# Second cross-attention: the values become TensorE's stationary operand, in four column tiles, and one matmul a pair adds and turns the partial results

## The reference, cut to what matters

```python
q = _fq_sym((x @ Wq + bq) * scale, axis=-1)     # 64 rows, 16 heads of 16
k = _fq_sym(k, axis=-1)                         # 6272 keys
v = _fq_sym(v, axis=2)
attn = softmax(einsum('bhqd,bhkd->bhqk', q, k))
attn = _fq_unsigned(attn, axis=-1)              # rounded to 255 steps of the row's maximum
out = einsum('bhqk,bhkd->bhqd', attn, v)
return out @ Wp + bp
```

## Time and profile before

| | us |
|---|---|
| median of three runs | 1012.08 (1010.8 to 1012.2) |
| the profiled execution's own time | 1010.85 |
| its span | 1009.0 |
| TensorE busy | 967.4 |
| VectorE busy | 714.2 |
| the stage of the change, first scores to `attended` | 293.1 to 372.2 |

### The profile page before, as it was taken

How to read it: one execution, slowest core, us unless ns; L and a number is a source line. 1 busy time by engine, 2 the same in 40 slices (tenths; PEclk the granted TensorE clock), 3 DMA queues, 4 the chain that set the end, 5 groups by cost and what they waited for, 6 DMA issues and landing times.

```text
span 1009.0 us, 20653 instructions
## 1 busy us (share of the span) xinstructions
PE 967.4 (96%) x7809; PEld 653.3 (65%) x7809; DVE 714.2 (71%) x1919; ACT 360.3 (36%) x629; POOL 163.4 (16%) x146
## 2 busy tenths in 40 slices
PE   9999999999799988998999999999999999998998
PEld 5676776776444554366777777777777777744555
DVE  5768776777789945788786767767676789753354
ACT  2332333324428841443343333333333343311211
POOL 0000000000210010234332323223322323000000
PEclk9999999999999989999999999999999999998999
DMA  8200100102439996990100000000000000413440
GB/s 319 75 22 23 40 21 21 42 5 85 151 127 183 192 300 240 352 315 3 41 12 1 2 0 0 0 0 0 0 0 0 0 22 22 168 63 99 165 179 3
DMA packets 70904, 82.99 MB, mean 82 GB/s; under 512 B 49728, under 2 KB 58176, under 8 KB 67008
## 3 DMA queue, kind: packets, MB, share of 16 engines
q1 hardware_dynamic: 70560, 82.17, 26.5%
q10 hardware_dynamic: 288, 0.07, 0.0%
HBM read 67.79 MB, written 2.42 MB: 70 GB/s over the span
## 4 chain that ended last, share of the span: by engine, by line
PE 76%; DVE 9%; issue 6%; DMA 3%; POOL 3%; ACT 3%; SPq 0%; POOLq 0%; DVEq 0%; PEld 0%; PEldq 0%
PE ps L2538 17%; PE ps L2429 13%; PE ps L2528 8%; PE ps L1682 8%; PE ps L1672 4%; PE ps L1693 4%; PE ps L1716 2%; PE ps L1728 2%; PE ps L532 2%; POOL x_sum L3114 2%; PE ps L3201 1%; DMA wide<-S 1%; DMA ring<-weights 1%; ACT S L2301 1%; PE ps L2452 1%
## 5 line engine op out<-in xcount | busy, mean ns | idle before, releaser
L2538 PE MATMUL ps<-vals,S 128*128 128x257 f32 x784 | 186.4, 381 | 1.0 <-ACT S L3043 1.0
L3114 POOL TENSOR_TENSOR x_sum<-x_max,consts 128x4 f32<-128x4 f32 (+1 forms) x104 | 136.1, 1309 | 298.6 <-DVE x_max L2748 298.6
L2538 PEld LDWEIGHTS ps<-vals,S 128*128 128x128 f32 x784 | 141.7, 190 | 18.8 <-issue 1.5
L2429 PE MATMUL ps<-keysT,row_biases_sb 128*128 128x512 f32 (+1 forms) x348 | 153.7, 568 | 0.0
L2760 DVE SCALAR_TENSOR_TENSOR S<-ps,x_sum,keysT 128x128 f32<-128x128 f32 x392 | 110.8, 344 | 55.4 <-PE ps L2538 50.9
L3043 ACT ACTIVATE S<-S 128x512 f32<-128x512 f32 (+1 forms) x104 | 62.6, 605 | 197.1 <-DVE S L2801 196.6
L2528 PE MATMUL ps<-x_q,x_keys 128*128 128x128 f32 x784 | 112.9, 286 | 0.0
L2528 PEld LDWEIGHTS ps<-x_q,x_keys 128*128 128x128 f32 x784 | 95.4, 191 | 0.1
L2429 PEld LDWEIGHTS ps<-keysT,row_biases_sb 128*128 128x128 f32 x348 | 62.8, 189 | 46.6 <-issue 41.9
L1682 PE MATMUL ps<-ring,S 128*128 128x512 f32 x196 | 92.4, 593 | 0.2
L1809 ACT ACTIVATE S<-ps 128x2048 f32<-128x2048 f32 (+1 forms) x25 | 46.1, 1844 | 82.7 <-PE ps L1728 76.5
(11 more groups left out here) (494 smaller groups left out, 1404.4 us busy)
## 6 DMA issues: line engine op xcount, KB each, us to landing
ring<-weights SPq DMA_DIRECT2D x24, 1024.0 KB, 6.9
keysT<-ctxT SPq DMA_DIRECT2D x2, 3136.0 KB, 15.8
vals<-ctxN SPq DMA_DIRECT2D x1, 6272.0 KB, 26.5
S<-ctxT SPq DMA_DIRECT2D x11, 512.0 KB, 4.0
ring<-weights SPq DMA_DIRECT2D x5, 768.0 KB, 6.0
kept_keys<-S SPq DMA_DIRECT2D x9, 256.0 KB, 2.7
x_keys<-kept_keys SPq DMA_DIRECT2D x9, 256.0 KB, 2.6
keysT<-weights SPq DMA_DIRECT2D x1, 1792.0 KB, 8.7
```

Source lines behind the costliest of these rows:

```text
L2429: ins = pe.matmul(ps[:, x2_key_bank(g, c), 0:width(c)], weights_of(g)[:, k, :], ctxT[:, k, span(c)], start=k == 0, stop=k == KT - 1)
L2538: ins = pe.matmul(bank(6, D + 1), S[:, a:a + TILE], ctx_and_ones[:, SUB * c + s, :], start=c == 0 and s == 0, stop=c == NC - 1 and s == su ...
L3114: pool.tensor_tensor(x2_inv[:, c % 2, 0:n], x2_var[:, c % 2, 0:n], C("neg_half").broadcast_to([128, n]), ALU.pow)\
```

## The change

In `weigh`, the stationary operand is now the pair's 32 value columns of a key tile (128 keys x 32) and the moving one the turned probabilities (128 keys x 128 queries). Key tile s goes to column tile s mod 4 of TensorE, that is to PSUM partitions 32 (s mod 4) and up. So four partial sums of 32 value columns x 128 queries stand below one another. The number of matmuls is the same.

`finish(j)` copies all 128 x 128 of them to one of two buffers `x1_parts`. A new TensorE step `fold(j)` takes this copy as stationary operand and `x1_fold` (four 32 x 32 identities below one another, f32) as the moving one: it adds the four partial sums and turns the result to 128 queries x 32, in its own place of bank 6 or 7. `fold(j-2)` stands ahead of `scores(j+1, 2)`, `fold(6)` inside `turn_last(2)`, and `fold(7)` after the last `weigh`. GpSimd makes `x1_fold` with two additions at the start of the stage. The last products read PSUM, and are four instead of two.

```diff
+            def fold(j):
+                pe.wait_ge(sem("x1_tile_done"), j + 1)
+                return pe.matmul(ps[:, 6 + j % 2, x1_own(j)], x1_parts[j % 2], x1_fold, start=True, stop=True)
...
             def turn_last(e):
...
                     if b == 6:
-                        pe.wait_ge(sem("x1_tile_done"), PAIRS - 1)
+                        fold(PAIRS - 2)
...
                 for s in range(n):
-                    ins = pe.matmul(ps[:, 6 + j % 2, 0:128], probsT[:, s, :], vals_int[:, x1_tile(e, s), 128 * (j // 4):128 * (j // 4) + 128],
-                                    start=e == 0 and s == 0, stop=e == PROB_GROUPS - 1 and s == n - 1)
+                    c = 32 * (s % 4)
+                    ins = pe.matmul(ps[c:c + 32, 6 + j % 2, 0:128], vals_int[:, x1_tile(e, s), 32 * j:32 * j + 32], probsT[:, s, :],
+                                    start=e == 0 and s < 4, stop=e == PROB_GROUPS - 1 and s >= n - 4, skip_group_check=True)
...
             pe.wait_ge(sem("values_narrowed"), 9)
+            pe.wait_ge(sem("x1_ident"), since("x1_ident", 3))
             for j in range(PAIRS):
                 if j == PAIRS - 1:
                     pe.wait_ge(sem("x1_scores"), since("x1_scores", PARTS * PAIRS))
+                if j >= 2:
+                    fold(j - 2)
...
             for e in (2, 3):
                 weigh(PAIRS - 1, e)
+            fold(PAIRS - 1).then_inc(sem("x1_weighed"), 1)
...
             def finish(j):
                 dve.wait_ge(sem("x1_weighed"), since("x1_weighed", PROB_GROUPS * (j + 1)))
-                dve.tensor_scalar(x1_out[:, 32 * j:32 * j + 32], ps[:, 6 + j % 2, 32 * (j % 4):32 * (j % 4) + 32], 2.0 ** 24, None, ALU.mult).then_inc(sem("x1_tile_done"), 1)
+                dve.tensor_scalar(x1_parts[j % 2], ps[:, 6 + j % 2, 0:128], 2.0 ** 24, None, ALU.mult).then_inc(sem("x1_tile_done"), 1)
...
-            dve.wait_ge(sem("x1_tile_done"), PAIRS)
+            dve.wait_ge(sem("x1_weighed"), since("x1_weighed", PROB_GROUPS * PAIRS + 1))
...
             for e in range(2):
                 rows_, cols_ = slice(T * e, T * e + T), slice(HD * e, HD * e + HD)
-                ins = dve.tensor_tensor(out[:, :, cols_], by_tile[rows_, :, cols_], step[rows_, :, cols_], ALU.mult)
+                for p in range(2):
+                    ins = dve.tensor_tensor(out[:, :, p, cols_], by_pair[rows_, :, p, cols_], step[rows_, :, p, cols_], ALU.mult)
...
+            pool.tensor_tensor(x1_fold64, C("ident")[:, 0:64], C("ident")[:, 64:128], ALU.add).then_inc(sem("x1_ident"), 1)
+            pool.wait_ge(sem("x1_ident"), since("x1_ident", 2))
+            pool.tensor_tensor(x1_fold, x1_fold64[:, 0:32], x1_fold64[:, 32:64], ALU.add).then_inc(sem("x1_ident"), 1)
```

More of the change, by code:

```diff
@@ L391, in perceiver @@
             "probsT_psum": (("x1_last_psum", 3, 7), ("x3_probsT_psum", 9, X3_PAIRS + 1)),
-            "probsT_ready": (("x1_ident", 3, 1), ("x3_probsT", 9, X3_PAIRS + 1)),
-            "weighed": (("x1_weighed", 3, PAIRS * PROB_GROUPS), ("x2_weighed", 6, GROUPS * NC), ("x3_weighed", 9, X3_PAIRS + 1)),
+            "probsT_ready": (("x1_ident", 3, 3), ("x3_probsT", 9, X3_PAIRS + 1)),
+            "weighed": (("x1_weighed", 3, PAIRS * PROB_GROUPS + 1), ("x2_weighed", 6, GROUPS * NC), ("x3_weighed", 9, X3_PAIRS + 1)),
             "tile_ready": (("x1_tile_ready", 3, 2), ("x2_tile_ready", 6, 2 * GROUPS)),
@@ L2031, in perceiver @@
         x1_queries = x2_probsT[:, :, :].rearrange("p a n -> p (a n)")
-        x1_q, x1_out = sw_key_both[0:T, 0, :], sw_key_both[:, 1, :]
+        x1_q = sw_key_both[0:T, 0, :]
+        x1_parts = [sw_key_both[:, 1, 128 * i:128 * i + 128] for i in range(2)]
+        x1_fold64, x1_fold = sw_value_part[:, 128:192], sw_value_part[:, 192:224]
         x1_q_rows = scratch(0, 1024, T)
@@ L2051, in x1_last_bank, with x1_own @@
             return 6 + (j + 1) % 2
+        def x1_own(j):
+            return slice(128 + 32 * (j // 2), 160 + 32 * (j // 2))
         def x1_probs(j, e):
@@ L2182, in x1_tensor @@
                     elif j + 1 == PAIRS:
-                        if e == 0:
-                            pe.wait_ge(sem("x1_ident"), since("x1_ident", 1))
                         turn_last(2 + e)
@@ L2280, in x1_vector @@
             finish(PAIRS - 1)
-            dve.wait_ge(sem("x1_tile_done"), PAIRS)
-            out, step = cut(attended[:, :], PAIRS, 32), cut(value_step[:, :], PAIRS, 32)
-            by_tile = cut(x1_out, PAIRS, 32)
+            dve.wait_ge(sem("x1_weighed"), since("x1_weighed", PROB_GROUPS * PAIRS + 1))
+            out = attended[:, :].rearrange("t (j p d) -> t j p d", p=2, d=32)
+            step = value_step[:, :].rearrange("t (j p d) -> t j p d", p=2, d=32)
+            by_pair = ps[:, 6:8, 128:256].rearrange("t p (j d) -> t j p d", d=32)
             for e in range(2):
                 rows_, cols_ = slice(T * e, T * e + T), slice(HD * e, HD * e + HD)
-                ins = dve.tensor_tensor(out[:, :, cols_], by_tile[rows_, :, cols_], step[rows_, :, cols_], ALU.mult)
+                for p in range(2):
+                    ins = dve.tensor_tensor(out[:, :, p, cols_], by_pair[rows_, :, p, cols_], step[rows_, :, p, cols_], ALU.mult)
             ins.then_inc(sem("attended"), 1)
```

## The result

The median went from 1011.44 us (four executions of each kernel, 1010.45 to 1012.2) to 1021.0 (1020.38 to 1022.49): 0.8% slower, ratio 1.0083 [1.0053, 1.0113]. That is 9.2 us above the forecast of 1011.8 and outside its range, the wide one of 1009.2 to 1014.8 too. The profiled execution took 1022.49 us, 11.64 more than the one of before. The ratios of this document leave out executions that took over 1.5% more than the fastest of the same kernel; of these eight none did.

What follows compares the result with a forecast made beforehand. Transposing transfers, 2.05 us each, were taken to bound the stage's middle, the TensorE chain and VectorE its end. Middle nothing, end -1.14, tail +0.82, sum -0.3: 1010.55 for the profiled execution, plus 1.23 for the median, 1011.8 us; range 1010.5 to 1012.6.

Steps and rivals of the forecast that it cites:

- the wide one: Range for the whole kernel's time, extended to the points of the three rivals: 1009.2 to 1014.8 us.
- The middle costs nothing: Middle of the stage: 1.3 us a pair less TensorE work changes nothing, hidden under transposing transfers at 2.05 us each.
- Rival 2: Middle of the stage: longer TensorE gaps drop the clock to 1.2 GHz, 1.7 us lost in each of two pairs; 1014.7; chance 0.18.
- The weighing (part 1): Each `weigh` of 12 or 13 matmuls: 0.35 us at full clock instead of 0.67, and 0.45 at the low one.
- Rival 3: Every `weigh`: loads of 32 columns don't overlap, so 0.67 us stays and only costs are left; +2.8, 1014.9; chance 0.06.
- The fold (part 2): Eight folds on TensorE, priced from a 0.34 us row; the middle's new wait free, 0.3 us fitting into the 1.3 saved.
- `finish` (part 3): VectorE's copy of 128 columns instead of 32: 0.28 us instead of 0.19, +0.08 eight times, under the transfers in the middle.
- The end (part 4): Stage end from 360.36 us: shorter weighing brings `finish(7)` 1.14 us earlier, the new tail takes back 0.82; sum -0.3.
- The tail: Stage end from `finish(7)`: longer copy +0.08, fold with hops +0.44, four products instead of two +0.30, together +0.82 us.
- The chain: TensorE's weighings and fillers from 360.36 us, then VectorE's copies: copies start 0.77 us earlier, `finish(7)` 1.14 us earlier.
- Rival 1: Middle of the stage: TensorE, not the queue, releases the scores, so shorter weighing gains; with the end -2.7, 1009.4; chance 0.15.
- Copies 0.8 us earlier: Sign that the forecast is right: VectorE's copies at the end of the stage start 0.8 us earlier in the profile after.

Runs made afterwards that it cites:

- e3_filled: Changed kernel with six whole-array filler matmuls of 128 columns behind each weighing up to `weigh(6, 0)`, some sums lost: median 1014.15 us, ratio 1.0013, two executions near 1030 left out.
- e5_three: Kernel before, old form of weighing, only the last three key tiles of each part weighed, the others left out: 1014.98 us, ratio 1.0021.
- e6_gap: Kernel before with one long wait in the middle: `weigh(2, 0)` waits until its pair's third transfer has landed; 1016.66 us, ratio 1.0044.
- e1_quarter: Kernel before, old form of weighing, nine of each part's 12 or 13 key tiles weighed, the others left out: 1011.03 us, ratio 0.999.
- e2_thrice: Changed kernel with the column-tiled matmuls of each part up to `weigh(6, 0)` issued three times, some sums lost: 1019.52 us, ratio 1.0069.
- e4_kept_warm: Kernel before with eleven filler matmuls of 512 columns in TensorE's idle stretch between `weigh(6, 0)` and `weigh(6, 1)`: 1011.5 us, ratio 0.9999.
- e7_three_fill: Changed kernel, all sums kept, three filler matmuls of 128 columns behind each weighing up to `weigh(6, 0)`: median 1029.11 us; ratio 1.0043 over the four executions up to 1020.33.
- e8_fill_and_end: Changed kernel, all sums kept, six fillers behind each middle weighing and eleven ahead of `weigh(6, 1)`: median 1028.07 us; ratio 1.0049 over the first six executions.
- e12_last_pair_held: Kernel before with column tiles and fold for pair 7 alone, its other products ahead of `finish(7)`, eleven fillers before `weigh(6, 1)`, six before the fold: 1011.19 us, ratio 0.9997.
- e10_burst: Changed kernel with one burst of 64 filler matmuls of 128 columns behind `weigh(3, 3)`: 1022.44 us, one execution.

## Why the prediction was wrong, point by point

**The middle costs nothing: this step failed.** "I cost it at nothing: the cover is the transfer queue" is true of the time that the work occupies, and `e3_filled` shows it as far as one execution can (2.08 us a transfer, stage -0.7 us). It missed that the hidden matmuls did something else: they kept TensorE's clock up. With them gone the clock fell in the middle of the stage (after; `e5_three` in the old form as well), and a TensorE at half speed is slower than the queue that was to cover it: 2.45 us a part against 2.05.

**Rival 2 was the case, mis-sized.** It named mechanism, place and direction, had 0.18, and gave 1014.7. A part at the low clock was priced at 2.35 (1.9 and 0.45) and takes 2.45 (2.01 and 0.44); the fold and the extra score block were priced at 0.5 and take 0.57 (331.05 to 331.62) and 0.56 (333.48 to 334.04). So a pair at its steadiest costs 2.7 us and not 1.7. The larger miss is the count: two pairs, while four paid, 2.3 us each. I had priced a fall and let the clock come back, as it does at the end of the stage before. But that return, and the one in `e6_gap`, came with the old weighing, the first with fillers too. The new mix doesn't lift the clock in 47 us (323.6 to 370.4) in which TensorE has no gap. Rival 2 also had the gaps grow "towards 2 us"; the clock fell behind one of 1.3, while one of 1.70 in `e1_quarter` left it up.

**The weighing (part 1).** Taken 0.35 us at full clock and 0.45 at the low one. Measured 0.28 from start to the next start ahead of a fold (321.44 to 321.72) and 0.44 (325.70 to 326.14), both with a change of tiling behind them, which the prediction added apart; without it 12 take 0.18 (`e2_thrice`). Rival 3 is ruled out.

**The fold (part 2)** waits for nothing in the middle, as said, and takes 0.34 at full clock (321.72 to 322.06). At the end `fold(5)` did wait, 1.53 us for `finish(5)` (371.95), in a place where TensorE waited 2.72 us for a landing before.

**`finish` (part 3)** takes 0.29 us, forecast 0.28.

**The end (part 4).** The tail from `finish(7)` to the end of `attended` is 1.52 us (381.32 to 382.84), 0.71 longer than before, forecast 0.82: the products cost less than the 0.22 each. The chain ahead of it is 1.83 shorter counted from the last transfer, forecast 1.14; that execution reached its end at a low clock, so the two can't be compared term by term. In `e3_filled`, with the clock up until about 361, near where it falls in the kernel before, the stage came out at -0.7, forecast -0.3.

**Rival 1**, a gain in the middle, had the transfers closer together. No run shows that beyond scatter: with the clock up they are 2.01 (`e1_quarter`) to 2.08 us apart (`e3_filled`, and `e4_kept_warm` with the old middle), and `e1_quarter` is at 0.999 [0.9973, 1.0006]. The one execution of `e5_three` at 1008.17 us leaves room for it.

**What the profile was to show.** A granted clock under 1 between 310 and 357 was named as the sign of rival 2, and it is what the stretches show. Copies 0.8 us earlier didn't come. The wide range was to reach to rival 3's point, which is 1014.9 and not 1014.8; nothing hangs on that.

**Left open.** Why one wait brings the clock down and a longer one in another kernel doesn't. Whether column-tiled work counts for less towards the clock than whole-array work does (`e2_thrice` leans to yes, `e5_three` shows that it isn't needed). What decides between the executions of one program in `e3_filled`, `e7_three_fill` and `e8_fill_and_end`. Where, behind the stage, `e12_last_pair_held` gives back its 2.7 us.

## What to carry to other kernels

Matmuls hidden under another engine's or a queue's pace are not free to remove: before taking them out, compare the pace that TensorE would have at half clock (2.45 us a part here) with the pace of what hides it (2.05). Where the first is longer, every part at the low clock costs the difference, and how many parts there are depends on whether what is left on TensorE is dense enough to bring the clock back: the old mix did so in 3.4 us (`e6_gap`), the new one not in 47 us without a gap. So price such a rival to the end of the stage, unless the rows show a reason for the way back.

## What the runs showed of the hardware that was not expected

- The clock can fall behind an idle stretch and not only in it: 1.32 us of waiting ended at 321.44, and it fell near 323.6 (1.52 us, 326.83 and 328.3 in `e5_three`). In the kernel before it fell within the wait. Waits of 1.25 us (`e2_thrice`) and 1.70 us (`e1_quarter`) were followed by no fall until the next long one.
- A TensorE that the profile shows busy 8.00 of 8 us can stay at 1.2 GHz for 47 us (323.6 to 370.4; 54.5 us in all until the clock was back). The Trainium skill (TensorE: Matmul & The Clock Gate, Part 1: The HAM clock gate) says that activity lifts the throttle. The burst of `e10_burst` and the old weighing of `e6_gap` agree; the rows at 8.00 of 8 and 0.50 show that a full busy time in the profile is no sign that the clock will rise.
- The same program has executions that keep the clock and others that don't: `e7_three_fill` spans 1010.91 to 1033.52 us. The mean granted clock nearly orders them (0.989 and 0.979 to 0.981 up to 1020.33 us, 0.958 to 0.966 from 1028.98 on), so it is to be read before any time is explained.
- The first transfer of the stage comes at 303.7 to 304.7 us in some executions and at 306.1 to 306.4 in others, with the same work before it. A single profile's span can't tell 2 us.
